# A two-layer attention and mixture-of-experts kernel: gates over 128 partitions, row maxima in two bf16 parts, weighted sums in three wide operations

## The reference

```python
x = L0_attn_x
xn = _layernorm(x)
x = x + _L0_attn_ref(xn, ...) + _L0_ffn_ref(xn, ...)
xn = _layernorm(x)
x = x + _L1_attn_ref(xn, ...) + _L1_ffn_ref(xn, ...)
...
# layer 0 attention: 16 heads of size 8
scores = jnp.einsum('bhqd,bhkd->bhqk', q, k) / SCALE
scores = jnp.where(causal_mask, jnp.float32(-1000000000000.0), scores)
probs = jax.nn.softmax(scores, axis=-1)
attn = jnp.einsum('bhqk,bhkd->bhqd', probs, v)
...
# layer 0 experts: 16, two for each token, hidden size 64, and one shared of 128
topk_p, topk_i = jax.lax.top_k(jax.nn.softmax(xf @ Wr, axis=-1), 2)
y = jax.nn.silu(xf @ wg) * (xf @ wu) @ wd        # for each expert
acc + y * c[:, None]                             # c: the token's share in it
```

## Time and profile before

| what | us |
|---|---|
| time before, median of 3 runs | 1806.54 |
| lowest and highest of them | 1803.79 and 1811.1 |
| profiled execution: span from first to last instruction | 1759.6 |
| PE busy in it | 1587.2 (90%) |
| DVE busy | 1401.9 (80%) |
| ACT busy | 955.8 (54%) |
| POOL busy | 915.0 (52%) |
| DMA, moved in it | 354.69 MB |

### The profile page before, as it was taken

How to read it: one execution, slowest core, us unless ns; L and a number is a source line. 1 busy time by engine, 2 the same in 40 slices (tenths; PEclk the granted TensorE clock), 3 DMA queues, 4 the chain that set the end, 5 groups by cost and what they waited for, 6 DMA issues and landing times.

```text
span 1759.6 us, 34071 instructions
## 1 busy us (share of the span) xinstructions
PE 1587.2 (90%) x12430; PEld 1099.6 (62%) x12430; DVE 1401.9 (80%) x2672; ACT 955.8 (54%) x1562; POOL 915.0 (52%) x973
## 2 busy tenths in 40 slices
PE   4899999889899999999989999999999999989950
PEld 2774555555566555445445877788888877778740
DVE  5779877677787878778796998888898899989942
ACT  2741556566666666555743556565555665535620
POOL 5207877651665475678776146622221365654256
PEclk9879999999999999999999999999999999999985
DMA  7963689989999776667448567665666577668413
GB/s 229 303 158 132 186 223 261 273 267 249 283 292 259 214 193 163 153 187 195 119 125 264 165 199 229 195 211 173 192 209 201 185 224 232 189 196 252 132 58 91
DMA packets 277959, 354.69 MB, mean 202 GB/s; under 512 B 32272, under 2 KB 204304, under 8 KB 272416
## 3 DMA queue, kind: packets, MB, share of 16 engines
q1 hardware_dynamic: 237600, 287.92, 57.1%
q0 software_dynamic: 17056, 33.66, 6.9%
q10 hardware_dynamic: 23136, 30.94, 5.1%
HBM read 197.48 MB, written 122.68 MB: 182 GB/s over the span
## 4 chain that ended last, share of the span: by engine, by line
PE 43%; DVE 23%; POOL 9%; issue 9%; DMA 7%; SPq 5%; ACT 4%; ACTq 0%; DVEq 0%; POOLq 0%
PE Y L1124 7%; PE R L867 5%; PE R L900 5%; PE R L869 5%; PE R L868 5%; POOL gat L1408 4%; DVE row_max L1997 3%; POOL xs_dram L1432 3%; DVE state L2098 3%; PE R L883 3%; PE Y L1018 2%; DMA q_rows<-kq 2%; DVE hid L2146 2%; DMA fw<-wf 2%; DVE dw L2092 1%
## 5 line engine op out<-in xcount | busy, mean ns | idle before, releaser
L1432 POOL DMA_INDIRECT xs_dram<-sc_in,pos x256 | 265.1, 1036 | 150.8 <-issue 58.7
L1408 POOL DMA_INDIRECT gat<-ys_dram,pos x256 | 262.6, 1026 | 125.3 <-issue 62.3
L1997 DVE TENSOR_REDUCE row_max<-R 128x6 f32<-128x768 f32 x256 | 238.9, 951 | 63.5 <-PE R L982 58.4
L900 PE MATMUL R<-ident_b 128*128 128x512 bf16 x936 | 255.8, 394 | 32.3 <-DVE K L1850 26.3
L1452 POOL TENSOR_TENSOR o_acc<-o_acc,read 128x512 f32<-128x512 f32 x112 | 146.1, 1304 | 263.8 <-DVE read L2108 262.7
L1124 PEld LDWEIGHTS Y<-fd,hid 128*128 128x128 f32 (+1 forms) x1824 | 232.3, 192 | 53.7 <-DVE hid L2146 25.9
L1604 ACT ACTIVATE probs<-R 128x768 f32<-128x768 f32 x256 | 203.8, 809 | 105.4 <-PE R L1006 99.2
L1124 PE MATMUL Y<-fd,hid 128*128 128x128 f32 (+1 forms) x1824 | 249.9, 280 | 11.3 <-DVE hid L2146 10.7
L1443 POOL TENSOR_SCALAR_AFFINE_SELECT probs<-probs 128x512 f32<-128x512 f32 x256 | 169.8, 664 | 158.1 <-ACT probs L1604 155.1
L867 PE MATMUL R<-fhl,fw 128*128 128x512 f32 x418 | 182.2, 436 | 1.3 <-DVE fhl L2136 1.3
L1723 ACT ACTIVATE sil<-R 128x512 f32<-128x512 f32 x190 | 112.9, 596 | 127.9 <-PE R L869 83.3
(11 more groups left out here) (270 smaller groups left out, 3399.6 us busy)
## 6 DMA issues: line engine op xcount, KB each, us to landing
fw<-wf SPq DMA_DIRECT2D x38, 1408.0 KB, 7.8
q_rows<-kq SPq DMA_DIRECT2D x128, 256.0 KB, 5.1
fx<-xs_dram SPq DMA_DIRECT2D x86, 256.0 KB, 3.4
xs_dram<-gat SPq DMA_DIRECT2D x24, 512.0 KB, 4.9
qk_dram<-qk_parts SPq DMA_DIRECT2D x32, 384.0 KB
Q<-qk_dram SPq DMA_DIRECT2D x64, 192.0 KB
...
```

The source lines that it names most:

```text
L900: pe.matmul(psum["R"][:, b * C:(b + 1) * C], ident_b[:, :], ident_b[:, :].unsqueeze(1).to_broadcast([P, TILES, P]), start=True, stop=True)
L1408: pool.indirect_dma_start(gat[:, i % 2, 2 * t + a, :], None, ys_dram[l][g], bass.IndirectOffsetOnAxis(ap=pos[l][g][a][:, col:col + 1], axi ...
L1432: pool.indirect_dma_start(xs_dram[g], bass.IndirectOffsetOnAxis(ap=pos[l][g][a][:, col:col + 1], axis=0), sc_in[:, n % 2, t * P:(t + 1) * ...
L1997: dve.tensor_reduce(row_max[:, b, h2, :, :], pair[:, :].rearrange("p (g c t) -> p g c t", g=2, t=P)[:, :, 0:3, :], AX.X, ALU.max).then_inc ...
```

## The change

Four edits. FU0: the gate matmuls of both blocks are written to one half of the bank's columns, block 0 in partitions 0 to 63 and block 1 in 64 to 127, the up matmuls likewise to the other half, so tanh, silu and product work on 128 partitions and 256 columns. BM: the maxima are kept by part, and split in two bf16 parts and not three, by three operations. `weigh`: all eight gathered tiles are multiplied with their shares in one operation, pairs added in a second, the other summand in a third. And C1b waits for the transpose of the chunk before. The planner's costs are set to 0.8, 0.3, 0.9, 3.4 and 1.9 us for what is shortened, by which it lays all lists out anew.

```diff
-ST_ROWS = QK_ROWS + 3
+MAX_PARTS = 2
+ST_ROWS = QK_ROWS + MAX_PARTS
...
-            stage(t + 1, "FU0", f, after=[("FT0", f, 0, "ACT")], PE=1.04, ACT=(whole, since(f, 2, ("FD0", 0, "PE"))),
-                  DVE=(1.5, since(f, 2, ("FD0", 0, "PE"))))
+            stage(t + 1, "FU0", f, after=[("FT0", f, 0, "ACT")], PE=1.04, ACT=(0.3, since(f, 2, ("FD0", 0, "PE"))),
+                  DVE=(0.8, since(f, 2, ("FD0", 0, "PE"))))
...
-                      DVE=(1.5, since(n, 1, ("BM", b, "PE"))), PE=0.25,
+                      DVE=(0.9, since(n, 1, ("BM", b, "PE"))), PE=0.25,
...
-                  + since(n, 1, ("C1b", 0, "ACT"), lag=stored), DVE=4.0, POOL=pow4)
-            stage(t + 16, "C1b", n, after=[("C1", n, 0, "POOL")], DVE=0.1, ACT=2.1)
+                  + since(n, 1, ("C1b", 0, "ACT"), lag=stored), DVE=3.4, POOL=pow4)
+            stage(t + 16, "C1b", n, after=[("C1", n, 0, "POOL")], DVE=0.1, ACT=(2.1, since(n, 1, ("C2", 0, "PE"))))
...
-            stage(t + 10, "E1", n, after=[(("EL", n, 0, "SP"), soon), (("EG", n, 2 * TILES - 1, "POOL"), soon)], DVE=2.4)
+            stage(t + 10, "E1", n, after=[(("EL", n, 0, "SP"), soon), (("EG", n, 2 * TILES - 1, "POOL"), soon)], DVE=1.9)
...
-                    for s in range(2):
-                        to = slice(s * S, (s + 1) * S)
-                        ins = pe.matmul(bank[:, to], fw0[:, n % F0_BUFS, s, 0:2 * F0], fT0[:, par, to], start=True, stop=True)
+                    for i in range(2):
+                        for s in range(2):
+                            ins = pe.matmul(bank[F0 * s:F0 * (s + 1), S * i:S * (i + 1)],
+                                            fw0[:, n % F0_BUFS, s, F0 * i:F0 * (i + 1)],
+                                            fT0[:, par, S * s:S * (s + 1)], start=True, stop=True)
...
-                    for g in range(2):
-                        sp.dma_start(Q[64 * g + QK_ROWS:64 * g + ST_ROWS, par, :, to],
-                                     max_rows[3 * H2 * g:3 * H2 * (g + 1), to]).then_inc(max_loaded.sem(2 * n + k), 16)
+                    for c in range(MAX_PARTS):
+                        sp.dma_start(Q[QK_ROWS + c::64, par, :, to],
+                                     max_rows[2 * H2 * c:2 * H2 * (c + 1), to]).then_inc(max_loaded.sem(2 * n + k), 16)
...
-                    act.activation(hid0[0:F0, par, :], bank[0:F0, :], ACT.Tanh, scale=0.5).then_inc(f0_tanh.sem, 1)
+                    act.activation(hid0[:, par, 0:S], bank[:, 0:S], ACT.Tanh, scale=0.5).then_inc(f0_tanh.sem, 1)
...
                         wait(*x1n_saved(n - 1))
+                        wait(*bank_of["xT1", n - 1].filled())
...
-                for a in range(2):
-                    for t in range(TILES):
-                        to = slice(t * P, (t + 1) * P)
-                        ins = dve.scalar_tensor_tensor(out=dst[:, to], in0=gat[:, i % 2, 2 * t + a, :],
-                                                       scalar=wt[l][g][a][:, at + t:at + t + 1],
-                                                       in1=(src, dst)[a][:, to], op0=ALU.mult, op1=ALU.add)
-                    if a == 0:
-                        link(ins)
-                return ins
+                rows = gat[:, i % 2, :, :]
+                shares = wt[l][g][:, at:at + TILES, :].rearrange("p t a -> p (t a)")
+                link(dve.tensor_tensor(rows, rows, shares.unsqueeze(2).to_broadcast([P, 2 * TILES, P]), ALU.mult))
+                pair = rows.rearrange("p (t a) d -> p a t d", a=2)
+                link(dve.tensor_tensor(pair[:, 0], pair[:, 0], pair[:, 1], ALU.add))
+                shaped = "p (t d) -> p t d"
+                return dve.tensor_tensor(dst.rearrange(shaped, d=P), pair[:, 0], src.rearrange(shaped, d=P), ALU.add)
...
-                    link(dve.scalar_tensor_tensor(out=upper, in0=lower, scalar=1.0, in1=bank[0:F0, :], op0=ALU.add,
+                    link(dve.scalar_tensor_tensor(out=grown, in0=gated, scalar=1.0, in1=bank[:, 0:S], op0=ALU.add,
                                                   op1=ALU.mult))
-                    dve.tensor_tensor(lower[:, 0:S], upper[:, 0:S], bank[F0:2 * F0, 0:S], ALU.mult)
-                    dve.tensor_tensor(upper[:, S:C], upper[:, S:C], bank[F0:2 * F0, S:C], ALU.mult).then_inc(bank.free, 1)
+                    dve.tensor_tensor(gated, grown, bank[:, S:C], ALU.mult).then_inc(bank.free, 1)
...
-                dve.tensor_reduce(row_max[:, b, h2, :, :],
+                dve.tensor_reduce(row_max[:, b, :, :, h2].rearrange("p c g -> p g c"),
...
-                    dve.tensor_scalar(neg[:, 0, :, :], by_head[:, :, :, 0], -1.0, None, ALU.mult)
-                    link(dve.tensor_tensor(rest[:, 0, :, :], by_head[:, :, :, 1], by_head[:, :, :, 2], ALU.max))
-                    link(dve.tensor_scalar(neg[:, 1, :, :], rest[:, 0, :, :], -1.0, None, ALU.mult))
+                    link(dve.tensor_tensor(peak[:, 1], peak[:, 1], peak[:, 2], ALU.max))
...
-                    link(dve.tensor_copy(parts[:, :, :, 0, :], neg))
-                    link(dve.tensor_tensor(rest, neg, parts[:, :, :, 0, :], ALU.subtract))
-                    link(dve.tensor_copy(parts[:, :, :, 1, :], rest))
-                    dve.tensor_tensor(parts[:, :, :, 2, :], rest, parts[:, :, :, 1, :], ALU.subtract)\
+                    link(dve.tensor_scalar(parts[:, :, 0, :], peak[:, 0:2], -1.0, None, ALU.mult))
+                    dve.scalar_tensor_tensor(out=parts[:, :, 1, :], in0=peak[:, 0:2], scalar=-1.0, in1=parts[:, :, 0, :],
+                                             op0=ALU.mult, op1=ALU.subtract).then_inc(max_split.sem, 1)
```

27 lines of the change are left out of this document (12 added, 15 removed).

## The result

After takes 1821.63 us (median of 5 runs, 1818.1 to 1827.08), before 1806.52 (5 runs): ratio 1.0098, 95% interval 1.0071 to 1.0125. I had forecast 1786.5 with a range to 1812. The change makes this kernel 1% slower.

The account below looks back on a forecast made before the run. It took no engine as full before 860 us, with VectorE's waits on the chain and GpSimd and DMA as second limits. Stretches of -7, -4, -5.5, -5.5 and +2 made -20: span 1739.6, time 1786.5 us, range 1766 to 1812.

Parts of the forecast that it names:

- What bounds the kernel: Engine limits read by stretch: no engine full from 150 to 860 us; what the change can win lies before 960.
- Part 1, row maxima: BM, 32 times: 0.75 us for three operations, 1.18 less each; 19.5 us on the path, part lost to GpSimd.
- forecast -7: Stretch 150 to 270 us: -8.0 from the row maxima, one of it lost to GpSimd.
- the -5.5: Stretch 610 to 860 us: -8.2 + 0.4, with 2.1 of BM's gain lost where GpSimd has a tenth left.
- BM's -3.3: Row maxima's gain in the middle: -2.0 us from 270 to 440 and -1.3 from 440 to 610.
- Part 2, gates: FU0, 48 times: VectorE -2.9 and -7.0 us, ScalarE's tanh -0.4 and -1.0, TensorE's shape change +4.5.
- The drain: FU0's changed matmul shape costs TensorE 0.25 us a tile, 12 us in all, +4.5 us on the path.
- Part 3, weighted sums: C1 and E1, 16 times each: three steps take 2.66 us, slower than the eight; +1 and +2 us on the path.
- Part 4, the order: Instruction order moves with the planner's costs, 27 of 936 fillers go; carries the saving to TensorE, no term of its own.
- Rival (d): Order counts 3.4 us of VectorE for C1 where 4.0 stood and sums grow: 15 us lost, 1802 to 1812; chance 0.06.
- Rival (b): GpSimd and DMA hold the pace, VectorE's saving becomes waiting: 0 to -9 us, 1798 to 1807; chance 0.22.
- The 46.9 us around the span: Runs' median above the profiled span of 1759.6 us, taken as start and end around it and left unchanged.

Follow-up runs that it names:

- e13: The kernel before, unedited, run again on the quicker chip: 1749.99 us, ratio 0.9993 to before.
- e16: Before with only the new weighted sums, in the old order: 1750.90 us, 1.0007 of before.
- e9: All new instructions of after with the planner's costs, and so the order, of before; a repeat on a second chip: 1744.99 us, 0.9965 of before.
- e10: Before with only the new row maxima (two bf16 parts, three operations), in the old order: 1742.10 us, 0.9952 of before.
- e15: Before with only the new gates (128 partitions), in the old order: 1747.29 us, 0.9974 of before.
- e14: The kernel after, unedited, run on the quicker chip: 1757.56 us, 1.0037 of before.
- e17: After with the planner's costs of C1 and E1 put back to 4.0 and 2.4 us: 1742.92 us, 0.9954 of before.
- e2: Instructions of before (plus C1b's wait) with the planner's costs of after, so only the order is new: 1850.37 us, 1.0258 of before.
- e12: All new instructions in the old order, with GpSimd's causal masks cut down (output leaves the mask out): 1729.84 us, 0.9868 of before.
- e11: Before with GpSimd's causal masks cut down (output leaves the mask out): 1733.37 us, 0.9897 of before.
- e5: Before with the planner's VectorE cost of FU0 at 1.49 and not 1.5 us, no instruction changed: 1769.99 us, 1.0099 of before.
- e3: All new instructions of after with the planner's costs, and so the order, of before: 1795.23 us, 0.9972 of before.
- e8: Code of after; of its planner costs only C1's 3.4 and E1's 1.9 us, the rest of before: 1759.34 us, 1.0025 of before.
- e7: Code of after; of its planner costs only BM's 0.9 us, the rest of before: 1759.90 us, 1.0028 of before.

## Why the prediction was wrong, point by point

The distance between marks in the traces (us), which is how I judge the steps by stretch: the start of the last VectorE step of the BMs, the first `fz`, and the end. e13 to e16 are of one chip, e9 and e10 of another on which before takes the same:

| kernel | 1st to 8th BM | 8th to 19th | 19th to last | last BM to first fz | from there to the end |
|---|---|---|---|---|---|
| e13, before | 116.3 | 333.0 | 250.7 | 122.8 | 778.4 |
| e10, maxima | 111.2 | 338.0 | 244.4 | 124.7 | 778.6 |
| e15, gates | 116.8 | 331.3 | 251.8 | 123.8 | 780.2 |
| e16, sums | 115.3 | 333.8 | 249.9 | 121.0 | 782.1 |
| e9, all, old order | 109.3 | 335.3 | 247.0 | 121.9 | 783.7 |
| e14, after | 108.2 | 337.5 | 236.2 | 132.6 | 792.3 |
| e17 | 108.0 | 336.0 | 240.4 | 126.5 | 782.0 |

Single runs of one kernel spread by some 10 us (e13: 1746.4 to 1758.1), so differences of 3 us in a cell mean nothing, and one trace of each can't share out a difference of a few microseconds among the columns.

**What bounds the kernel.** Reading by stretch was right, but the sentence "what the change can win lies before 960" left out that it can lose behind it, and in e14 it lost most there (on the slower chip e2 lost before it). The order of after does win before (the 236.2 of the third column), and from its lead of 13.7 us at the last BM it falls 23.7 back, 9.8 of them by the first `fz` and 13.9 behind it.

**Part 1, row maxima.** Right by piece (0.74 us). By effect: -8.4 us (e10, interval 4.7 to 12.3) where 19.5 less 3 stood. In 150 to 270 most of the forecast -7 shows (116.3 to 111.2, and 109.3 in e9), and in 610 to 860 the -5.5 (250.7 to 244.4). In the middle, 270 to 610, BM's -3.3 does not show (333.0 and 338.0), though these two traces alone can't settle a term of that size. The wait itself did go. The weight loads of BM's transposes, e13 and then e9:

```profile
L990 PEld LDWEIGHTS R<-ident_b,max_parts 128*48 128x48 bf16 x64 | 4.0, 100 | 19.9 <-DVE max_parts L2012 15.7 <-issue 4.1
```

```profile
L991 PEld LDWEIGHTS R<-ident_b,max_parts 128*32 128x32 bf16 x64 | 4.0, 94 | 8.2 <-issue 8.0
```

TensorE waited 15.7 us for `max_parts` before and not at all after. Of these 15.7 the end saw half. The term that was mis-sized is the 19.5 us: multiplying a chain's 31.9 us by 0.61 takes each piece as time won; it is only time until the next thing is late. What that is in 150 to 270 the trace of e9 says:

```profile
150.00:270.00 120.00, 113.37 (x1334) 62.02 (x1332) 82.07 (x131) 64.54 (x99) 95.27 (x114) 0.97 0.74 195
```

TensorE is busy 113.4 of 120 us, up from 111.6 in e13, and 28.41 us of that are fillers, of which a list holds a fixed number:

```profile
150.00:270.00 120.00, 28.41 (x99) 8.25 (x97) 0.97 0.74 195
```

e12 agrees. The first column is 110.1 in e11 and 109.1 in e12: the light masks alone win 6.2 us there, the new instructions alone 7.0, and both together 7.2. That the fillers are what stops it was not tried.

**Part 2, gates.** Forecast -9.9 - 1.4 + 4.5 = -6.8 us, measured -4.5 (e15, interval -8.9 to -0.2): right in sum. The drain, 0.25 us a tile, was oversized. The gate and up matmuls in e13 and in e15:

```profile
L953 PE MATMUL R<-fT,fw 128*128 128x256 f32 x192 | 54.8, 409 | 1.0 <-DVE row_max L1997 0.4 <-ACT probs L1604 0.4 <-ACT fT L1572 0.2
...
L953 PEld LDWEIGHTS R<-fT,fw 128*128 128x128 f32 x192 | 34.3, 195 | 10.0 <-issue 2.9 <-ACT fT L1572 1.5 <-DVE row_max L1997 0.9
```

```profile
L953 PE MATMUL R<-fT,fw 128*64 128x256 f32 x384 | 53.3, 400 | 0.6 <-ACT probs L1606 0.4 <-DVE row_max L1998 0.2
...
L953 PEld LDWEIGHTS R<-fT,fw 128*64 128x64 f32 x384 | 23.7, 139 | 16.9 <-issue 5.7 <-ACT fT L1574 2.7 <-ACT probs L1606 0.6
```

Idle on "issue" before their weight loads went from 2.9 to 5.7 us in all, 0.06 us a tile and not 0.25, and the matmuls took 1.11 us a tile, not more. In the new order after (9.7) and e2 (3.3) are further apart, 0.13 us a tile. The Trainium skill (TensorEngine Tiling (Array Packing), Key Properties) has a drain whenever the tiling mode changes; here every tile changes the shape twice, and the traces leave room for 0.06 to 0.13 us a tile, not for the 0.25 that I took or the 0.33 of the one row behind it. With 2.8 us in all, 1 on the path, the sum would have been -10.3, outside the interval: so the saved steps gave less than their -11.3, and two errors cancelled. That the sum came out right is luck.

**Part 3, weighted sums.** Forecast +3, measured +1.2 (e16, -2.3 to +4.7). Undisturbed, the three take what I said; the tile `gat` in e14 (min, median, max in ns):

```profile
L1818 DVE TENSOR_TENSOR gat<-gat,wt x32: 1201/1225/2425, 459.0 to 1748.9; 128x1024 f32<-128x1024 f32 x32
L1820 DVE TENSOR_TENSOR gat<-gat x32: 691/692/1669, 460.2 to 1750.2; 128x512 f32<-128x512 f32 x32
...
L1822 DVE TENSOR_TENSOR acc_in<-gat,acc_in x16: 691/693/693, 1413.0 to 1750.9; 128x512 f32<-128x512 f32 x16
```

These medians make 1.225 + 0.692 + 0.693 = 2.61 us and two links. The mean over all, 2.95 in e14, is above it by single steps of up to 2.4 us, none of them in the last stretch; that it is GpSimd's work beside them was not tried. Why three are slower than eight the same rows tell. From 512 to 1024 columns a step grows from 0.692 to 1.225 us, 1.04 ns a column, which leaves 0.16 us that each step pays whatever its size. Eight old steps of 128 columns are then 8 x 0.16 + 1024 x 0.00104 = 2.34 us, and 2.31 was measured; three new ones 3 x 0.16 + 2048 x 0.00104 = 2.61. The Trainium skill's rule (VectorE: DVE Perf Modes, The TRN2 errata) that the fixed part is paid by each instruction holds: five steps fewer save 0.8 us. But a fused multiply and add went over each column once, and the new steps go over twice as many columns, which costs 1.07. The prediction's reason, that the eight hide most of their fixed part behind each other, is wrong, though its 2.66 us was about right.

**Part 4, the order.** This is the step that failed. I wrote of the new order that it "is how the saving reaches TensorE, no term of its own". It is the largest term: +46 us with the old instructions (e2), +12.6 us with the new ones (e14 against e9), and +17 from a cost changed by 0.01 (e5). The prediction took the order for free because it sits in no row of the trace. I read the old order and the new as two draws among many, which no reading of the old trace prices; what in the new lists makes them slower stays open. On the slower chip the loss sits between the 8th and the 19th BM (e2), on the quicker one behind the last BM (e14). C1b's wait was never tried alone; e3 and e9 have it and don't lose.

**Rival (d)** had the mechanism and its price (0.95 us x 16 = 15 us), and I gave it 0.06. e17 against e14 gives 0.8%, 14 us; e8 against e9, the same two costs in another surrounding, 0.6%. Two pairs with the same sign and size speak for it. Against it speak e5 and e7, which lose in layer 1 with the sums' true costs, and e2, which with the low ones doesn't (788.0, 787.6 and 781.0 us, one trace each). Since e5 shows that 1% can come from nothing, the pairs don't prove that a cost set too low is worse than one that is merely different, and this stays open. The profile did hold the hint: a cost had been lowered by 0.6 for a step that my own sum made longer.

**Rival (b).** e11 shows that shorter masks win 1%, e12 that GpSimd does not take VectorE's saving. Whether the DMAs, at a share of 0.90 to 0.93 in e9 to e16 there, hold 270 to 610 was not tried; the second column, which no part moved, would fit.

**The 46.9 us around the span.** A misreading. Spans lie 1.7 to 2.1 us under their own runs in all traces of the experiments. The trace of before was of an execution some 45 us quicker than the runs beside it, by its marks like those of the quicker chips, and I should have seen in this that its idle times might not be theirs. As the sum was a difference, it did not shift the ratio.
